# Gated cross-attention and an eight-expert layer: from ten turns in a ring of three to one list of slots, twelve per batch

## The reference

```python
x = x + tanh(g_xattn) * attention(layernorm(x), ctx)   # 16 heads of 16, queries from x, keys and values from ctx
x = x + tanh(g_ffn) * moe(layernorm(x))                # 8 experts, 256 x 256, top 1
# moe: logits = xt @ wg; the expert with the largest; a token's place is the number of earlier
# tokens (over all batches) of the same expert; places from 112 on are dropped;
# out = gate * (xt @ W[e].T + b[e])
```

## Time and profile before

| | us |
|---|---|
| median of 3 runs | 296.07 |
| lowest, highest | 293.12, 302.96 |
| profiled execution | 294.2 |
| its span (first to last instruction) | 292.5 |
| granted TensorE clock, mean | 0.819 of full |
| PE, DVE, ACT, POOL busy | 200.9, 139.9, 87.0, 63.5 |

### The profile page before, as it was taken

The page is one execution under the profiler, slowest core; times in us unless marked ns, Lnnn a source line. Parts: engine busy times, 40 slices in busy tenths (PEclk is TensorE's granted clock), DMA queues, the critical chain, the costliest instruction groups (busy, mean ns, idle before and its releaser), DMA issues. The chain is left out here.

```text
span 292.5 us, 4359 instructions
## 1 busy us (share of the span) xinstructions
PE 200.9 (69%) x1703; PEld 126.1 (43%) x1703; DVE 139.9 (48%) x311; ACT 87.0 (30%) x180; POOL 63.5 (22%) x67
## 2 busy tenths in 40 slices
PE   2685148399569975997399659957981998712590
PEld 1463024266335643554156326633640566512370
DVE  4179948248405731573167127622850764522270
ACT  1320030136122602360245125402531365400120
POOL 4439990011010101010101011001100201073064
PEclk9979558869977987699789859975995799965597
DMA  4979459806980895079409930990399948052731
GB/s 132 228 73 98 37 60 121 69 0 65 119 64 2 83 124 43 0 88 123 37 0 97 122 26 12 108 120 6 43 99 154 321 136 237 2 158 87 221 94 53
DMA packets 36840, 26.77 MB, mean 92 GB/s; under 512 B 15528, under 2 KB 34074, under 8 KB 36714
## 3 DMA queue, kind: packets, MB, share of 16 engines
q1 hardware_dynamic: 32453, 21.40, 59.7%
q10 hardware_dynamic: 3349, 2.67, 3.5%
q0 software_dynamic: 1024, 2.51, 2.8%
HBM read 9.25 MB, written 5.52 MB: 51 GB/s over the span
## 5 line engine op out<-in xcount | busy, mean ns | idle before, releaser
L848 DVE TENSOR_REDUCE nmax<-sc 112x1 f32<-112x375 f32 x128 | 67.2, 546 | 58.4 <-PE sc L442 57.5
L686 ACT ACTIVATE prob<-stp 128x448 f32<-128x448 f32 (+1 forms) x80 | 43.0, 542 | 69.1 <-PE stp L450 68.2
L442 PE MATMUL sc<-k,q 125*112 125x375 bf16 x128 | 45.7, 386 | 20.9 <-DMA k<-parts 15.9
L1007 POOL TENSOR_TENSOR parts<-rest,parts 128x487 bf16<-128x487 f32 x16 | 17.1, 1071 | 157.2 <-ACT parts L637 157.0
L408 PE MATMUL pj<-ctx_sb,wk_sb 128*128 128x375 f32 x64 | 35.0, 666 | 17.8 <-DMA ctx_sb<-in_ctxT 17.1
L450 PE MATMUL stp<-q,k 128*128 128x112 bf16 (+1 forms) x320 | 33.1, 238 | 14.6 <-DMA q<-mrows 14.6
L459 PE MATMUL pv<-prob,v_sb 128*32 128x112 f32 (+1 forms) x768 | 38.5, 281 | 0.4 <-ACT prob L686 0.3
L450 PEld LDWEIGHTS stp<-q,k 128*128 128x128 bf16 (+1 forms) x320 | 22.6, 124 | 27.2 <-issue 16.9
L442 PEld LDWEIGHTS sc<-k,q 125*112 125x112 bf16 x128 | 17.8, 149 | 31.6 <-DMA k<-parts 17.1
L839 DVE TENSOR_TENSOR rest<-pj,parts 128x487 f32<-128x487 f32 x16 | 10.5, 659 | 34.0 <-ACT parts L637 34.0
L459 PEld LDWEIGHTS pv<-prob,v_sb 128*32 128x32 f32 (+1 forms) x768 | 15.8, 111 | 23.7 <-issue 14.8
(11 more groups left out here) (100 smaller groups left out, 200.7 us busy)
## 6 DMA issues: line engine op xcount, KB each, us to landing
k<-parts SPq DMA_DIRECT2D x48, 187.5 KB, 7.3
q<-parts SPq DMA_DIRECT2D x48, 56.0 KB, 6.9
ctx_sb<-in_ctxT SPq DMA_DIRECT2D x8, 281.2 KB, 7.2
wT_sb<-in_wT ACTq DMA_DIRECT2D x1, 2048.0 KB, 14.7
slots<-xin SPq DMA_DIRECT2D x1, 1799.0 KB, 15.8
xin<-slots SPq DMA_DIRECT2D x8, 224.9 KB, 5.0
be_sb<-in_be SPq DMA_DIRECT2D x1, 896.0 KB, 6.1
x_sb<-in_x SPq DMA_DIRECT2D x1, 784.0 KB, 11.6
```

What stands on the lines that cost most here:

```text
L442: pe.matmul(sc[h % 2][0:NQ, 0:NK], q6[0:MAXROW, b3, h, :], k6[0:MAXROW, b3, h, :], start=True, stop=True).then_inc(s_sc, 1)
L686: nc.scalar.activation(prob[0:kn, n % 3, :], bank_of_sT(t, n)[0:kn, 0:4 * NQ], ACT.Exp, scale=SCALE).then_inc(s_p, 1)
L848: nc.vector.tensor_reduce(nmax[:, h:h + 1], sc[h % 2][0:NQ, 0:NK], axis=AX.X, op=ALU.max, negate=True).then_inc(s_max, 1)
L1007: ins = nc.gpsimd.tensor_tensor(parts[:, t % RING, 2, m, :], rest[:, m, :], parts[:, t % RING, 1, m, :], ALU.subtract)
```

## The change

```diff
-RING = 3
+KR = 3
+VR = 2
+TURN = 12
+S_AT = 0
+HEADS = ((0, 1), (2,), (3,), (4, 5), (6,), (7,), (8, 9), (10,), (11,), (12, 13), (14,), (15,))
+K_AT = -16
+KE_AT = (-14, -12)
+KSPLIT_AT = (-13, -11)
+LAY_AT = -7
+V01_AT, V01E_AT = 12, 16
+V2_AT, V2E_AT = 16, 18
+SPLITMAX_AT, MAXT_AT, MROW_AT = 13, 14, 15
+T_AT, PV_AT = 17, 18
+NORM_AT, WO_AT, ADD_AT = 30, 31, 32
+LN_AT, X2T_AT, LG_AT = 33, 35, 36
+QG = ((0, 1), (1, 5), (5, 8))
...
+            def lay_k(b):
+                if b >= KR:
+                    sp.wait_ge(s_st, UNITS * (b - KR + 1))
+                for part, ready in ((0, s_khi), (1, s_kmid), (2, s_klo)):
+                    sp.wait_ge(ready, 2 * (b + 1))
+                    for j in range(len(K_PART)):
+                        if K_PART[j] == part:
+                            sp.dma_start(k6_flat[HD * j:HD * (j + 1), b % KR, :],
+                                         parts_k[:, b % 2, part, :, :].rearrange("p m n -> p (m n)"))\
+                              .then_inc(s_klaid[b % 2], 16)
...
+            def scores(b, h):
+                if H * b + h >= 2:
+                    pe.wait_ge(s_max, H * b + h - 1)
...
+            for s in range(FIRST, LAST + 1):                      # PE
+                if s == 0:
+                    turn_xn(1)
+                    for m in range(2):
+                        project_q(1, m)
+                if (found := at(s, T_AT)):
+                    scores_T(*found)
+                if (found := at(s, S_AT)):
+                    scores(found[0], HEADS[found[1]][0])
+                if (found := at(s, K_AT, 4)) and found[0] > 0:
+                    project_k(*found)
+                if (found := v_at(s, V01_AT, 4)):
...
+                if (found := at(s, S_AT)):
+                    for h in HEADS[found[1]][1:]:
+                        scores(found[0], h)
+                if found := at(s, WO_AT, 1):
+                    through_wo(found[0])
+                if found := at(s, MAXT_AT, 1):
...
+                if found := at(s, PV_AT):
+                    probs_v(*found)
...
+            for s in range(FIRST, LAST + 1):                      # DVE
...
+                if found := at(s, NORM_AT, 1):
+                    normalise_pv(found[0])
+                if found := at(s, ADD_AT, 1):
+                    add_x(found[0])
...
+                if found := at(s, S_AT):
+                    for h in HEADS[found[1]]:
+                        take_max(found[0], h)
+                if s == 2:
+                    dve.wait_ge(s_x[2], 16)
+                    statistics(5, 8)
+                if s == 4:
+                    normalise(2)
...
+            for s in range(FIRST, LAST + 1):                      # POOL
+                if s == 2:
+                    for m in range(2):
+                        q_lo(1, m)
+                if s == 4:
+                    rstd(2)
+                if found := at(s, SPLITMAX_AT, 1):
+                    split_max(found[0])
+                for m in range(2):
+                    if (found := at(s, KSPLIT_AT[m], 1)) and found[0] > 0:
+                        k_split(found[0], m)
+                if s == 6:
+                    constants()
+                if s == 9:
+                    for m in range(2):
+                        q_lo(2, m)
+                    pool.wait_ge(s_tbo, 1)
+                    pool.wait_ge(s_xn, B)
+                    nc.gpsimd.tensor_tensor(x_sb[:, :, :], x_sb[:, :, :],
+                                            bo_sb[:, :].unsqueeze(1).to_broadcast([NQ, B, D]),
+                                            ALU.add).then_inc(s_xbo, 1)
+                    more_constants()
```

More of the change, by code:

```diff
@@ L275, in settle @@
[L275 to L296, removed]
@@ L380, in _ @@
+            sp.wait_ge(s_x1, B)
+            sp.dma_start(out_v[:, B - 1:B, :], rows[:, B - 1:B, X1:X1 + D]).then_inc(s_outx, 16)
+            sp.wait_ge(s_scat, 16 * B)
             for e in range(E):
@@ new lines, in places @@
+            def places(n, lo, hi):
+                pe.wait_ge(s_mask, n + 1)
+                if n == 0:
+                    pe.wait_ge(s_tri, 2)
+                    pe.wait_ge(s_max, H * B)
+                else:
+                    pe.wait_ge(s_slot, n)
+                for b in range(hi - 1):
+                    first_b = max(lo, b + 1)
+                    pe.matmul(sc[1][0:NQ, (first_b - lo) * E:(hi - lo) * E], every[:, :],
+                              maskb[:, b:b + 1, :].to_broadcast([NQ, hi - first_b, E]),
+                              start=(b == 0), stop=False, skip_group_check=True)
+                pe.matmul(sc[1][0:NQ, 0:(hi - lo) * E], before[:, :], maskb[:, lo:hi, :],
+                          start=False, stop=True, skip_group_check=True).then_inc(s_place, 1)
@@ L616, in _, with product @@
                 mm.then_inc(s_xinT, 1)
+            def product(e):
+                pe.wait_ge(s_xinTe, e + 1)
+                if e >= 2:
+                    pe.wait_ge(s_res, e - 1)
+                for c in range(2):
+                    mm = pe.matmul((misc, pv)[e % 2][0:CAP, 0:D], xinT[:, e, c, :],
+                                   wT_sb[:, e, c, :], start=(c == 0), stop=(c == 1))
+                mm.then_inc(s_y, 1)
+            pe.wait_ge(s_wk, 16)
+            pe.wait_ge(s_ones0, 1)
@@ L617, in _ @@
+            places(2, *R2)
+            pe.wait_ge(s_wT, 16 * E)
+            for e in range(E):
+                turn_xin(e)
                 if e:
@@ L960, in scatter, with rstd @@
-            def scatter(lo, hi):
-                for b in range(lo, hi):
-                    nc.gpsimd.indirect_dma_start(
-                        slots, bass.IndirectOffsetOnAxis(ap=slot[:, b:b + 1], axis=0), rows[:, b, :],
-                        None, bounds_check=SLOTS - 1, oob_is_err=False).then_inc(s_scat, 16)
+            link = Chain(pool, s_pchain)
+            def rstd(g):
+                lo, hi = QG[g]
+                pool.wait_ge(s_stat, g + 1)
+                link(nc.gpsimd.tensor_scalar(ve1[:, lo:hi], mv1[:, lo:hi, 1], EPS, None, ALU.add))
+                nc.gpsimd.tensor_tensor(rs1[:, lo:hi], ve1[:, lo:hi], half[:, lo:hi], ALU.pow)\
+                    .then_inc(s_rstd, 1)
@@ L966, in _, with scatter @@
+            def scatter(b):
+                nc.gpsimd.indirect_dma_start(
+                    slots, bass.IndirectOffsetOnAxis(ap=slot[:, b:b + 1], axis=0), rows[:, b, :],
+                    None, bounds_check=SLOTS - 1, oob_is_err=False).then_inc(s_scat, 16)
             link(nc.gpsimd.memset(ident[:, :], 0.0))
```

1145 lines of the change are left out of this document (548 added, 597 removed).

## The result

| | before | after |
|---|---|---|
| median | 298.8 us (4 runs) | 269.5 us (4 runs) |
| lowest, highest | 293.12, 302.96 | 263.21, 276.6 |
| profiled execution, its span | 294.2, 292.5 | 263.76, 261.7 |
| granted clock, mean | 0.819 | 0.778 |

The change makes the kernel faster: ratio 0.894, 95% interval 0.875 to 0.914. Against the 247 us forecast the 263.5 of the lower two is 16.5 us too many: inside the range, but above the 259 up to which the forecast's own terms reached.

The account below looks back on a forecast made before the run. PE, busy 69%, was taken to be held by three DMA waits (47.6 us) and the clock they lower. Head 65.5, slots 17 to 95 120, slots 96 to 113 22, tail 36.4: span 244, time 247 us; range 230 to 272.

Parts of the forecast that it names:

- Three waits go: PE's waits for the context tile, K's rows and the maxima's rows, 47.6 us together, were to vanish.
- K alone takes 5.7 us at 202 GB/s: Per-batch K copies, 1.15 MB, were to transfer in 5.7 us, hidden in the 12 us between release and use.
- Rival 2: Transfers still in the way: K's copies at about 90 GB/s, 3 us for each of five batches; 269 us, chance 0.11.
- The 8 us given to Q's short runs: Of about 14 us that K and Q copies took per turn before, Q's 224-byte runs were credited with 8.
- One slot, 0.90 us; a batch, 18 plus a stall: PE work in slots 17 to 95 at full clock, plus a 1.2 us wait per batch for maxima behind normalising.
- Rival 1: Hand-offs in every slot: PE waits for ScalarE's exponential, 0.2 us in each of 96 slots; 266 us, chance 0.12.
- The stretch starts cold, 1.5 us: Slots 17 to 95 were to lose 1.5 us to low clock at their start, within 120 us.
- Rival 3, the clock stays low: At 1.2 GHz a batch's 18 us of PE become about 31, 13 more; all of it low 350 us; chance 0.05.
- The head, 65.5: Start to slot 17: transposed scores begin at 65.5 us, after GpSimd's in-order chain; bounds 56 and 72 if transfers queue.
- The lock on each batch's product, left out: VectorE's two-SBUF-operand product might block behind GpSimd on the shared port, 6 us over eight batches; not in the sum.
- Slots 96 to 113, 22; tail 36.4: Last transposed scores and PV with final steps, 22 us; from last PV to the end, 36.4 us.

Follow-up runs that it names:

- q_again: attn_rows with the per-batch Q copies put back, six of 56 KB in 224-byte runs ahead of each batch's K copies; 281.9 us, ratio 0.955.
- split_norm: attn_head with VectorE's normalising cut in two, division behind that slot's maxima, Wo and what follows one slot later; 244.7 us.
- attn_rows: Changed kernel with only the attention matmuls (scores from batch 1 on, transposed scores) on 128 rows; 243.0 us, ratio 0.824.
- before_few_rows: Kernel before with scores on 96 rows instead of 125, transposed scores 99 instead of 128, K and V 96 and 97; 316.2 us, ratio 1.054.
- attn_head: attn_rows with GpSimd's fills held until VectorE has normalised, and its add and routing constants moved from slot 9 to 16; 244.5 us.
- head_free: Changed kernel, few rows kept, with GpSimd's fills held behind VectorE's normalising and its add and routing constants moved to slot 16; 262.7 us.
- queue_few: head_free with the third group's Q rows and the context tiles of batches 5 to 7 moved from slot 8 to 17 in SyncE's list; 260.3 us.
- proj_rows: Changed kernel with only the f32 projections of K and V on 128 rows; 249.4 us, ratio 0.846.
- queue_head: attn_head with the third group's Q rows and the context tiles of batches 5 to 7 moved from slot 8 to 17 in SyncE's list; 252.8 us.
- first_rows: attn_rows with 128 rows only in the first turn (slots 12 to 28), later matmuls on 96 to 99; 245.6 us, ratio 0.831.

## Why the prediction was right or wrong

- *Three waits go.* Right: 41.8 us to 4.6, none for context tiles after the start. The prediction's 47.6 counted as a turn's wait the 5.8 us at the very start, which no order of turns could take away.
- *K alone takes 5.7 us at 202 GB/s.* Wrong as a size. The 202 was one slice, at the start of a burst. With Q's copies gone K does not run at that rate. The bandwidth line from 107 to 182 us (slices of 1.9 us; among them the experts' weights):

```profile
DMA  0000039999920009999990001899996000399994
GB/s 0 0 0 0 14 101 152 120 122 126 189 93 0 0 6 160 117 127 118 123 243 19 0 0 34 177 117 118 123 121 219 9 0 6 78 146 115 116 116 56
```

  Most full slices move 115 to 127 GB/s, so 1.15 MB take some 9.6 us (an estimate from these slices). It still fits into the 12 us between release and use, with 2 us of latency just so. Rival 2 was nearer than its 0.11 says: q_again fell into it with six copies of 56 KB more per batch, and split_norm touched it. The 8 us given to Q's short runs are wrong as well: in q_again they added 3 to 4.
- *One slot, 0.90 us; a batch, 18 plus a stall.* Right: 18.28 us a batch at full clock, stall 0.77 for 1.2. Rival 1 did not come: PE waited 0.3 us in all for `prob`.
- *The stretch starts cold, 1.5 us.* This is the step that failed. At its place the clock was low for 36 us, and for 19 more from 185 on. In attn_rows the same slots took 118.0 us, after 137.5: 19.5 us more than with full rows, where the whole term was 1.5. Under it lay a premise that the prediction never wrote down: that a matmul on 96 to 99 rows costs what one on 125 to 128 costs. Per matmul at full clock it does (a score 0.32 to 0.34 us in the earlier trace rows, 0.33 after). It doesn't in how long PE stays at the lower clock.
- *Rival 3, the clock stays low.* It came in part, for 55 us and not for all; by its price, 13 us more for 18 of work, the 49 us beyond attn_rows' 6 are worth 49 x 13/31 = 20. Mechanism and price came true, though the price by luck: the K pair that it is said to come from (1.25 against 0.63) makes 36 us of 18, not 31. The chance of 0.05 was too low. The argument against it was the earlier trace rows: before paused 1.52 us and stood at 1.00. But that row was taken with 128 rows of operand. At that point of the same list before_few_rows, with 96 to 99, stands at the lower clock from 234 to 262 us.
- *The head, 65.5.* Walked nearly rightly (three normalisations 7.99 us beside fills of 7.96, until 44.8 where I had 44). Of the 3 us, 1.7 had come by the turning of the maxima (64.03, forecast 62.3), the other 1.3 behind it: 4.5 us to T where I had 3.2, 2.55 of them the wait for the rows. attn_head shows how full the queue was there; it was named as a bound and not taken. The normalisations are as long as the fills they stood beside, and 1.05 us without them: by the rule on the port pair in the Trainium skill (SBUF — State Buffer, Terms) the loser blocks for the full instruction, and both traces agree.
- *The lock on each batch's product, left out.* Right: that product takes 395 ns after as 393 before.
- *Slots 96 to 113, 22; tail 36.4.* 19.3 and 36.4. The last scatter stands at 237.56, 12.2 behind the last PV, where I had 12.1, and the end 24.1 behind it, where I had 24.3.

What stays open. The stretches at low clock with few rows ended 2 to 5 us behind the start of a Wo, whose matmuls have 128 rows: Wo at 100.15 and 199.15 after, at 100.32 in head_free, at 95.27 in queue_few, at 115.83, 172.74 and 259.02 in before_few_rows (its stretch from 197 to 231 ended right with one, at 230.38). That fits the theory but wasn't tried alone, and matmuls on 128 rows did not always bring the clock back: before_few_rows has eight of the Q projection, between 141 and 155 us, in a stretch that lasts to 176. And the fall at about 183 us after, behind a wait of 1.59 us for K, is no matter of rows: the same wait (1.57 to 1.59 us) was followed by a fall in proj_rows and, with many rows in T and the scores, in queue_head, and by none in attn_rows, attn_head and first_rows. What differs is again how long it lasts, 7 us in proj_rows and queue_head and 20 after. When such a wait drops the clock is not settled. All added rows hold zeros on one side, so it is the number of rows read that was tested, not their values.

## What to carry to other kernels

When an edit changes the shape of the matmuls, ask of the clock again: here, from the same point of the same list, PE stayed at half speed for 6 us with full operand rows and for 36 with a quarter of them missing, and looked 100% busy meanwhile. Filling operands up to 128 rows with zeros is cheap to try, and here twelve slots of it behind the pause were enough. When a wait is removed and the time stays, look what was waiting under it: here POOL's list, SP's queue and K's rows lay one behind the other, and moving a transfer out of one wait put it into the next.

## What the runs showed of the hardware

| busy PE at 0.50 behind a pause | rows of scores and T; of K's and V's projection | length, us |
|---|---|---|
| after, from 68.5; from 185 | 96 to 99; 96, 97 | 36; 19 |
| queue_few, from 60.7 | 96 to 99; 96, 97 | 37 |
| proj_rows, from 70.7; from 172.5 | 96 to 99; 128 | 6; 7 |
| attn_rows, from 68.6 | 128; 96, 97 | 6 |
| queue_head, from 60.1; from 89.8 | 128; 96, 97 | 6; 4 |

Copies of K from SBUF to SBUF into 16 partitions moved 115 to 127 GB/s in runs of 1500 bytes, not the 202 that one slice of before suggested. In q_again 107 to 130 went on with Q's runs of 224 bytes mixed in; the 69 to 118 of the earlier trace rows were measured where K's own runs had 750 bytes.
